# Value products issued two groups later in the attention of the last layer

## The reference, cut to what matters

```
def _L3_attn_ref(x, W_qkv, b_qkv, W_out, b_out):
    qkv = (x @ W_qkv + b_qkv).reshape(b, s, h, 3 * hd)
    q, k, v = qkv[..., :hd], qkv[..., hd:2 * hd], qkv[..., 2 * hd:]
    logits = jnp.einsum('bshd,bkhd->bhsk', q, k) / np.sqrt(hd)
    logits = jnp.where(k_pos > q_pos, -jnp.inf, logits)
    attn = jax.nn.softmax(logits, axis=-1)
    out = jnp.einsum('bhsk,bkhd->bshd', attn, v).reshape(b, s, d)
    return out @ W_out + b_out
...
for e in range(E):                       # experts, in _L3_ffn_ref
    h = new_gelu(x_flat @ w1[e].T + b1[e])
    output = output + cw[:, e:e + 1] * (h @ w2[e].T + b2[e])
...
x = x + _L3_attn_ref(xn, ...) + _L3_ffn_ref(xn, ...)
```

## Time and profile before

| | |
|---|---|
| runs of the kernel before | 2266.69, 2266.37, 2261.76 us |
| span of the profiled execution, first to last instruction | 2265.1 us |
| what the median has beyond that span | 1.3 us |
| TensorE, VectorE, ScalarE, GpSimd busy over the whole span | 83%, 79%, 61%, 57% |
| last layer's attention, from the first reduction of maxima to the end | 1553 to 2265 us |
| a slot with four expert tiles, three tiles, none (slots 13, 11, 15) | 45.4, 41.3, 31.2 us |
| TensorE's idle time before its instructions, slots 4 to 13 (466 us) | about 54 us |

### The profile page before, as it was taken

One profiled execution on the slowest core, in us unless ns is written; L12 is line 12 of the kernel. 1 busy time (PEld: TensorE's weight loads), 2 busy tenths in 40 slices (PEclk: granted clock), 3 DMA queues, 4 the chain that ended last, 5 costly groups with the idle time before them and its releaser, 6 DMA issues. The chain is left out here.

```text
span 2265.1 us, 32659 instructions
## 1 busy us (share of the span) xinstructions
PE 1884.8 (83%) x10276; PEld 999.3 (44%) x10276; DVE 1796.7 (79%) x2181; ACT 1381.4 (61%) x2604; POOL 1293.2 (57%) x954
## 2 busy tenths in 40 slices
PE   5798988889898987788985899955688988888886
PEld 5333333334343433344662688842244544445432
DVE  6699999899989999967879899868656665566673
ACT  2666767666767675465353787631476666766666
POOL 5689999999999999801333445446511111111265
PEclk6999999999999999899987899955899999999998
DMA  3355444445545555420030000022422332223112
GB/s 77 109 157 152 156 146 158 149 153 161 159 146 159 152 157 158 134 86 30 1 91 0 1 0 0 0 62 82 120 67 76 111 107 83 80 84 108 57 34 76
DMA packets 156309, 217.53 MB, mean 96 GB/s; under 512 B 31722, under 2 KB 68602, under 8 KB 155546
## 3 DMA queue, kind: packets, MB, share of 16 engines
q1 hardware_dynamic: 152074, 207.41, 30.3%
q0 software_dynamic: 4096, 8.40, 1.4%
HBM read 196.59 MB, written 23.86 MB: 97 GB/s over the span
## 5 line engine op out<-in xcount | busy, mean ns | idle before, releaser
L1035 POOL TENSOR_TENSOR m_dBx<-m_du,m_rowB 128x1024 f32<-128x1024 f32 x256 | 603.8, 2386 | 9.9 <-DMA m_rowB<-bc_rows 9.8
L758 PE MATMUL ps<-m_hC,ident 128*128 128x512 f32 x1024 | 517.2, 652 | 104.5 <-DVE m_hC L1117 104.2
L3195 DVE TENSOR_REDUCE a_mx<-ps 128x2 f32<-128x1024 f32 (+2 forms) x320 | 350.8, 1117 | 141.3 <-PE ps L2757 105.0
L2985 ACT ACTIVATE a_pT<-ps 128x512 f32<-128x512 f32 (+2 forms) x640 | 318.7, 558 | 225.6 <-PE ps L2780 199.4
L934 ACT ACTIVATE ps<-m_delta,m_A 128x512 f32<-128x512 f32 x512 | 332.8, 682 | 144.9 <-DVE m_hC L1117 113.1
L758 PEld LDWEIGHTS ps<-m_hC,ident 128*128 128x128 f32 x1024 | 205.4, 208 | 398.9 <-issue 238.3
L3356 POOL TENSOR_SCALAR_AFFINE_SELECT a_pT<-a_pT 128x512 f32<-128x512 f32 x104 | 66.1, 635 | 431.1 <-ACT a_pT L2985 430.8
L1117 DVE TENSOR_TENSOR m_hC<-ps,m_rowC 128x1024 f32<-128x1024 f32 x176 | 215.4, 1224 | 16.7 <-issue 1.3
L1108 DVE TENSOR_TENSOR_SCAN ps<-ps,m_dBx 128x1024 f32<-128x1024 f32 x88 | 201.1, 2285 | 30.0 <-POOL m_dBx L1035 16.6
L1045 POOL TENSOR_TENSOR m_hC<-m_h,m_rowC 128x1024 f32<-128x1024 f32 x80 | 194.6, 2432 | 45.2 <-DVE m_h L1108 45.0
L1108 DVE TENSOR_TENSOR_SCAN ps<-ps,m_carry,m_dBx 128x1024 f32<-128x1024 f32 x88 | 206.4, 2345 | 5.4 <-ACT m_dBx L959 4.5
(11 more groups left out here) (410 smaller groups left out, 3510.9 us busy)
## 6 DMA issues: line engine op xcount, KB each, us to landing
m_rowB<-bc_rows SPq DMA_DIRECT2D x256, 256.0 KB, 3.9
m_rowC<-bc_rows SPq DMA_DIRECT2D x256, 256.0 KB, 3.4
a_w<-in_L3f_w1T SPq DMA_DIRECT2D x39, 256.0 KB, 2.8
a_w<-in_L3f_w2T SPq DMA_DIRECT2D x39, 256.0 KB, 3.7
expert_rows<-in_zero_rows SPq DMA_DIRECT2D x39, 128.0 KB, 2.7
a_xs<-expert_rows SPq DMA_DIRECT2D x39, 128.0 KB, 2.9
expert_out<-a_y SPq DMA_DIRECT2D x39, 128.0 KB, 3.6
qk_parts<-a_part SPq DMA_DIRECT2D x18, 256.0 KB
```

Source lines behind the costliest of these rows:

```text
L758: mm = pe.matmul(ps[:, bankY + c, :], k.ident[:], hC[:, n % NBUF, c, :], start=False, stop=n % NS == NS - 1)
L1035: pool.tensor_tensor(dBx[:, n % NBUF], du[:, i % 2, :, chunk(i, x)], rowB[:, n % 4, :].unsqueeze(1).to_broadcast([P, HALF, CH]), ALU.mult) ...
L2985: act.activation(dst, src, ACT.Exp).then_inc(t_read, 1)
L3195: dve.tensor_reduce(mx[:, c % 2, :, es[0]:es[0] + len(es), t, x // CH], src, AX_X, ALU.max)\
```

## The change

A slot is now cut into 48 **places**, four to a group, and tables say at which place each piece of work is issued; all engines and the ring tables read the same tables. scoreT(g,0) and the group's first S have the group's first place, scoreT(g,2) and the second S the third. Most tables repeat the old order. What differs:

- In slots 0 to 15 sums(g) has place 4(g+2)+1, that is, the second quarter of group g + 2 and ahead of scoreT(g+2,2); sums(9) and sums(10) follow at the end of group 11, and sums(11) in the next slot as before. In slots 16 to 18 the sums stay one group behind.
- XT follows the group's second S, where it stood ahead of it.
- Z comes after the first scoreT and the first S of a slot, where it was first.
- On ScalarE, out(c, 0) comes after the burst's gelus, since sums(3) is now issued in group 5.
- In slots 5 and 9 VectorE divides the sums (X) ahead of the last subtraction of the projection, not behind it.

`pT` keeps its three buffers and `exps` its wait.

```
-SHARE = (2, 2, 1, 1, 2, 2, 2, 2, 2, 2, 1, 1)
-BURST = 4
+PLACES = 4 * GROUPS
+SCORES_AT = (0, 2, 4, 6, 8, 12, 16, 18, 20, 22, 24, 26, 28, 30, 32, 34, 36, 38, 40, 44)
+ROWS_AT, DOWN_AT = (2, 6, 10, 14), (31, 35, 39, 43)
+UP_AT = (19, 19, 19, 19, 19, 19, 19, 19)
+PARTS_AT = (7, 11, 15, 19, 23, 27, 31)
+MAX_AT, SPLIT_AT = (0, 0), (0, 0)
+SUMS_AT = (9, 13, 17, 21, 25, 29, 33, 37, 41, 45, 47), \
+    (6, 10, 14, 18, 22, 26, 30, 34, 38, 42, 46)
+LAST_SUMS_AT = 1, 2
+COPY_AT = (19, 3), (19, 3)
...
                 for s in range(SLOTS + 1):
...
-                        if back:
-                            scoreT(b, g, 0)
-                        for i in units[:1]:
-                            score(f, i)
...
-                        if back and g > 0:
-                            sums(b, g - 1)
...
+                    for place in range(PLACES):
+                        g, quarter = divmod(place, 4)
+                        if 0 <= b < NI and quarter in (0, 2) and pair_of(g, quarter):
+                            scoreT(b, g, quarter)
+                        for i in scored(s, place):
+                            score(s, i)
+                        for kt, x in ups_of(s, place):
+                            up(kt, x)
+                        for c, x in summed(s, place):
+                            sums(c, x)
+                        for kt in rows_of(s, place):
+                            turn_rows(kt)
...
+                        if max_turned(s, place):
+                            turn_max(s - 1)
...
             @block.scalar
...
+                        if 0 <= c < NI and quarter in (0, 2):
+                            exps(c, g, quarter)
+                        for kt, x in ups_of(s, place):
...
+                            gelu(kt, x)
+                        for x, half in halves(s, place, COPY_AT):
+                            out(x, half)
```

More of the change, by code:

```diff
@@ L2893, in _ @@
                 for s in range(SLOTS + 1):
[L2894 to L2900, removed]
-                            scoreT(b, g, 0)
-                        for i in units[:1]:
-                            score(f, i)
-                        if back and not front and len(TU[g]) > 2:
-                            scoreT(b, g, 2)
-                        if back and g > 0:
-                            sums(b, g - 1)
[L2908 to L2917, removed]
@@ L2918, in _ @@
                             count()
-                        for x, part in projected(s, g):
+                        for x, part in projected(s, place):
                             project(x, part)
[L2921 to L2935, removed]
             @block.scalar
@@ L3275, in _ @@
                 for s in range(SLOTS + 1):
[L3276 to L3281, removed]
-                            largest(first, i)
[L3283 to L3288, removed]
+                    first = s
+                    for place in range(PLACES):
+                        for i in scored(s, place):
+                            largest(first, i)
+                        for kt in rows_of(s, place):
+                            rows_turned(kt)
+                        for kt in downs_of(s, place):
+                            down_done(kt)
+                        if max_turned(s, place):
+                            turned_max(s - 1)
+                        for c, half in halves(s, place, TURN_AT):
+                            norm(c, half)
+                        for x, u in by_batch(s, place, MERGE_AT):
+                            out_turned(x, u)
+                        for x, u in by_batch(s, place, OUT_AT):
+                            residual(x, u)
+                        if s == 0 and place == 3:
                             slots()
-                        for x, part in projected(s, g):
+                        for x, part in projected(s, place):
                             if part == 2:
@@ L3375, in _ @@
                 for s in range(SLOTS):
-                    if 0 <= s - 1 < NI:
-                        split_max(s - 1)
                     if s < 2:
                         for i in range(len(SU)):
+                            if s == 1 and i == sum(p <= MAX_AT[0] for p in SCORES_AT):
+                                split_max(0)
                             pool.wait_ge(s_read, s_at["S", s, i] + 1)
```

151 lines of the change are left out of this document (81 added, 70 removed).

## The result

The changed kernel took **2287.0 us** (median of four runs, 2283.0 to 2293.2) against 2266.5 for the kernel before (four runs): a ratio of 1.0105, with a 95% interval of 1.0083 to 1.0128. It is slower, by 20.5 us where 6.0 were forecast, and outside the range.

A forecast was written before the change was run, and what follows sets the result against it. TensorE, issuing in order, was taken to bound the kernel: its work plus about 5 us of waits a slot. From 2266.4 us, +0.8 for waits and +5.2 for the clock gave 2272.4 us, range 2260 to 2280.

The forecast's parts named there:

- The slot boundary: Start of a slot: scoreT(0,0) and S0 cover Z's wait for the reduction of maxima, 1.12 us gained.
- Groups 0 to 3: Slot's front: mask waits go, 2.0 us of VectorE waits come; burst 16.8 us after previous slot's S18 (the mark), no change.
- The burst's exit: Behind the burst: scoreT(5,2) waits some 2.7 us for copy and table load, not 1.01; 0.55 us a slot lost.
- the gain inside the burst: Inside the burst: TensorE's waits fall from 0.78 to some 0.33 us, so scoreT(5,0) comes 0.45 us earlier.
- Waits over the slots: Sum over the last layer's slots: +4.7 us in slots 4 to 13, -0.4 and -3.5 elsewhere, +0.8 us in all.
- The walk: Slot-by-slot sum of changed waits, without the clock: 4.7 - 0.4 - 3.5 = +0.8 us.
- A slot 15 that does not shrink: Sign of being wrong: slot 15 was to take 2.3 us less, its mask waits of 2.9 us mostly going.
- The clock: Slots 4 to 13: the clock falls in four of the six slots spared before, 1.3 us each, +5.2 us.
- The reading that the term rests on: Slots 4, 5, 7 and 9 before: each clock fall followed the burst and then the wait for ScalarE.
- the clock falling in every slot: Rival for slots 4 to 13: all six spared slots fall too, 2275.9 us, or 2279 with more ring waits; chance 0.15.
- The other side: Rival in groups 0 to 2: S2 waits under 0.2 us for VectorE, so about 2256 us; chance 0.15.

The follow-up runs named there:

- e1: The changed kernel with sums(3) ahead of the burst and the copy of the first half ahead of the gelus again: 2275.5 us.
- e3: The changed kernel with scoreT(5,0) repeated eight times behind sums(3) in slots 3 to 13: 2270.5 us.
- e5: Against the kernel before with Z alone moved (2265.4 us): sums(3) and later sums two groups behind, copy behind the gelus: 2305.5 us.
- e10: The changed kernel with scoreT(5,0) repeated four times behind sums(3): 2284.4 us.
- e8: Against the kernel before with Z alone moved (2265.4 us): scoreT(5,0) repeated four times between S8 and sums(4) in slots 4 to 13's range, slots 3 to 13: 2266.0 us.

## Why the prediction was wrong

- **The slot boundary, right.** Z's wait went, to 0.9 us in ten slots (0.53 of it in slot 13).
- **Groups 0 to 3, right.** S2 was to wait about 0.75 and XT1 0.55 for VectorE; slot 13 shows 0.66 and 0.53. The burst was to begin 16.8 us after the mark: 2117.22 - 2100.38 = 16.84. In that the number is better than its written sum: 15.3 and 2.0 of new waits make 17.3, and the step down to 16.8 is not explained. What the scores had waited for VectorE before, 4.4 us in ten slots, would have to come off the 2.0 and bring it to 16.9.
- **The burst's exit, right in kind, a little small.** The wait of scoreT(5,2) was to be 2.7 and is 2.71. It comes 2129.18 - 2117.22 = 11.96 us after the burst's start, where 11.7 was forecast and 11.15 stood before: 0.8 a slot lost and not 0.55. The term that was too large is the gain inside the burst, 0.45: the waits there went from 0.78 to 0.53 only. The first load begins 1.21 us after the burst's start (2118.43 - 2117.22) where it was 1.45 (2106.76 - 2105.31), 0.24 earlier and not 0.6; in front of it now stand 0.24 us of "issue", for which the profile names no releaser.
- **Waits over the slots, right in sum, in part by luck.** The walk gave +4.7 us for slots 4 to 13; their waits grew by 5.1. Slot by slot they changed by -0.5 (slot 9) to +1.3 us (slot 4), and the exit alone, at 0.8 a slot, would have made 8. The walk gave -3.0 for slots 14 and 15; the waits listed there fell from 12.5 to 9.5 us. All the same slot 15 grew, from 31.20 to 31.96 us. A slot 15 that does not shrink was one of the prediction's own signs of being wrong. Its waits did fall, from 7.5 to 5.6 us; its busy time rose from 23.61 to 26.37 us, which is the next point.
- **The clock, wrong: this is the step that failed.** "I expect it to fall in four of the six that were spared: 4 x 1.3 = +5.2". It fell in all six, it cost more in several of them (slot 11 has 2.46 us more of busy time, slots 6 and 10 have 2.7 and 2.6, against my 1.3), it went lower in slots that had fallen before (slot 7 from 0.96 to 0.92), and it fell in slots 14 and 15, to which I gave no such term because they have no burst. TensorE's busy time rose by 15.0 + 5.4 = 20.4 us, four times the term: about 12 in the six spared slots, about 3 in the four others, 5.4 in slots 14 and 15. The waits' balance of both stretches, 5.1 - 3.0, is near the walk's. I treated the fall as an event with a fixed price at one place. The runs showed it at several places, more than once in a slot: a second time in slots 5 and 9 of the changed kernel, twice each in slots 14 and 15, and at the front of the slot in e1, e3, e5 and e10.
- **The reading that the term rests on, half wrong.** "What those four did before the fall was the same each time: the burst, and then the wait for ScalarE." That holds for slots 4 and 7 of the kernel before. In slots 5 and 9 the clock stayed full behind the burst and fell some ten us later, where TensorE had waited for VectorE twice. Slot 5, timeline of TensorE, then two stretches, the first of which begins with the burst's exit (columns as above):

```profile
1754.72 0.39 PE L2752 MATMUL ps<-a_k,a_q 48*128 48x512 bf16 x2 [1.07 <-DVE a_att L3215]
1755.86 3.48 PE L2843 MATMUL ps<-a_w,a_h 128*128 128x128 f32 x16 [0.74 <-DVE a_mx L3195]
```

```profile
1745.00:1753.00 8.00, 4.98 (x46) 1.73 (x46) 4.70 (x5) 7.24 (x13) 0.00 (x0) 1.00 0.00 0
1756.00:1759.00 3.00, 3.00 (x16) 3.00 (x16) 0.93 (x1) 0.65 (x1) 0.00 (x0) 0.54 0.01 3
```

So two of the four falls of the kernel before did not stand behind the wait that the change makes longer.

- **The rivals.** The nearest was the clock falling in every slot, 2276 to 2279; it had the mechanism, and it too was short for slots 14 and 15, for the deeper falls and for a second fall in a slot. The Trainium skill, in "TensorE: Matmul & The Clock Gate", section on HAM oscillation, tells of matmuls that are slowed again at every pass; the ten slots below 1.00 of the changed kernel agree, the six at 1.00 of the kernel before do not. The other side, VectorE's reads not deciding, wanted S2 to wait under 0.2 us; in slot 13 it waited 0.66.

## What to carry to other kernels

Removing waits of TensorE at two places and making one longer wait at a third can cost more than the sum of the waits says: look what the clock does behind the longest one, and hold TensorE's busy time for the same products before and after against each other, for that is the clock's price without any model. An operation that stands behind another engine's work (here the copy behind the gelus, and the table load behind the copy) should be moved ahead of it before anything is delayed into it. Delay a product by what its input needs (here half a group), not by a whole step of the loop, and if an idle stretch can't be removed, repeating a product into a bank that nobody may read yet can be worth its time: it was behind a wait of 2.7 us (e3), and it was not shown to be behind one of 1 us (e8).

## What was not expected of the hardware

- 1.8 us of useless products a slot made the kernel 16.5 us faster (2287.0 to 2270.5), and 0.9 us made no difference (2284.4).
- The switch of ScalarE's table took 1.28 us and nothing beside it: the copy ends at 2126.54 + 0.59 = 2127.13, the load begins at 2127.14, and the first exponential behind it at 2128.44.
- The same wait behind the burst, 2.7 us, went with a clock of 0.94, 0.95 and 0.92 in three kernels; what stands in the front of the slot counts too.
- Where idle time was taken away or left at one place, falls came up at another: none at the front of the slot in the changed kernel, five in e3 and six in e10, whose fronts are the same. Which idle time of a slot brings which fall stays open.
